# An expert stage on one core: in each slot the first-layer matmuls ahead of the second-layer matmuls of four slots back

## What is computed

```python
x = x + _L0_ffn_ref(_L0_cond_ref(x, cond, ...), ...)
# layer 1, the recurrence:
xw = einsum('ntd,dh->nth', x, Wx) + b
next_h = tanh(xw_t + prev_h @ Wh)               # 128 steps
# layer 1, the experts (E = 8, H = 128, F = 512):
router_logits = einsum('bth,eh->bte', x, router_w)
topk_values, topk_indices = top_k(router_logits, 2); topk_weights = softmax(topk_values)
h1 = gelu(einsum('bth,efh->btef', x, w1) + b1)
expert_outputs = einsum('btef,ehf->bteh', h1, w2) + b2
x = x + sum(topk_weights * take(expert_outputs, topk_indices))
```

## Time and profile before

| | us |
|---|---|
| median of 3 executions (305.28 to 305.82) | 305.47 |
| the profiled execution's own time | 305.9 |
| its span, first to last instruction | 304.1 |
| PE busy, 87% of the span | 265.9 |
| DVE busy, 85% | 259.6 |
| ACT busy, 71% | 216.3 |

### The profile page before, as it was taken

One profiled execution on the slowest core, in us unless ns is written; L12 is line 12 of the kernel. 1 busy time (PEld: TensorE's weight loads), 2 busy tenths in 40 slices (PEclk: granted clock), 3 DMA queues, 4 the chain that ended last, 5 costly groups with the idle time before them and its releaser, 6 DMA issues.

```text
span 304.1 us, 8645 instructions
## 1 busy us (share of the span) xinstructions
PE 265.9 (87%) x2716; PEld 205.2 (67%) x2716; DVE 259.6 (85%) x635; ACT 216.3 (71%) x455; POOL 74.6 (25%) x148
## 2 busy tenths in 40 slices
PE   4969950059989999999999999999999999999994
PEld 4724450026956877778888788888777877877873
DVE  4888999989898897879887789987789988899885
ACT  5368899997842667767777566667566766778882
POOL 3368996000025402010311122311110201101000
PEclk9979965558999999999999999999999999999999
DMA  6990544002500000000000001000001000001000
GB/s 178 325 300 4 98 95 77 8 0 52 88 0 2 1 2 1 0 2 9 11 0 0 2 2 29 0 0 0 1 2 28 8 0 0 2 1 38 0 2 26
DMA packets 24031, 10.62 MB, mean 35 GB/s; under 512 B 13356, under 2 KB 22983, under 8 KB 24007
## 3 DMA queue, kind: packets, MB, share of 16 engines
q1 hardware_dynamic: 23470, 10.05, 13.6%
q10 hardware_dynamic: 536, 0.26, 0.3%
HBM read 6.11 MB, written 1.05 MB: 24 GB/s over the span
## 4 chain that ended last, share of the span: by engine, by line
PE 74%; ACT 12%; DVE 8%; DMA 2%; issue 2%; ACTq 0%; DVEq 0%; SPq 0%
PE bank L891 73%; ACT big L518 2%; ACT big L516 2%; ACT big L525 2%; ACT big L521 2%; ACT big L532 2%; DMA wn<-in_w_gate 2%; DVE peak L631 1%; DVE big L742 1%; DVE wyT L825 1%; DMA y_sb<-in_cond 1%; ACT xT L466 1%; DVE big L870 0%; PE bank L1015 0%; DVE big L744 0%
## 5 line engine op out<-in xcount | busy, mean ns | idle before, releaser
L891 PE MATMUL bank<-big,wt 128*128 128x384 f16 (+2 forms) x480 | 124.7, 336 | 0.0
L891 PE MATMUL bank<-wt,big 128*128 (+1 forms) x1536 | 112.8, 219 | 1.4 <-DVE big L870 0.9
L870 DVE TENSOR_TENSOR big<-big 128x384 f16<-128x384 f32 (+2 forms) x160 | 93.3, 585 | 22.3 <-ACT big L592 18.2
L891 PEld LDWEIGHTS bank<-wt,big 128*128 128x128 f16 x1536 | 97.1, 97 | 19.8 <-issue 3.7
L590 ACT ACTIVATE big<-bank,miscT 128x384 f32<-128x384 f32 (+2 forms) x160 | 96.3, 603 | 11.2 <-PE bank L891 9.6
L891 PEld LDWEIGHTS bank<-q,wxh 128*128 128x128 f32 x254 | 44.8, 190 | 16.7 <-issue 2.8
L580 ACT ACTIVATE q<-bank (+1 forms) x112 | 20.6, 184 | 45.2 <-PE bank L891 44.4
L891 PEld LDWEIGHTS bank<-big,wt 128*128 (+1 forms) x480 | 49.6, 117 | 3.3
L404 POOL CAST big<-q 128x64 f16<-128x64 f32 x32 | 13.5, 423 | 133.3 <-ACT q L580 130.8
L866 DVE CAST big<-big 128x512 f16<-128x512 f32 (+2 forms) x104 | 38.8, 373 | 5.1 <-ACT big L590 4.6
L825 DVE SCALAR_TENSOR_TENSOR wyT<-bank,gates,wyT 128x128 f32<-128x128 f32 x128 | 39.8, 343 | 1.0 <-PE bank L891 0.4
(11 more groups left out here) (165 smaller groups left out, 312.4 us busy)
## 6 DMA issues: line engine op xcount, KB each, us to landing
wnat<-in_w SPq DMA_DIRECT2D x8, 512.0 KB, 7.7
x_sb<-in_x SPq DMA_DIRECT2D x4, 256.0 KB, 4.5
out_block<-wyT SPq DMA_DIRECT2D x15, 64.0 KB
wn<-in_w_gate ACTq DMA_DIRECT2D x1, 192.0 KB, 5.0
wn<-in_w_up SPq DMA_DIRECT2D x1, 192.0 KB, 5.9
wn<-in_w_down SPq DMA_DIRECT2D x1, 192.0 KB, 5.9
b_in<-in_b SPq DMA_DIRECT2D x12, 4.0 KB
wt<-wyT SPq DMA_TRANSPOSE x8, 3.0
```

What stands on the lines that cost most here:

```text
L870: V.tensor_tensor(g_lo[:, par, f, 0:w], g32[:, f, 0:w], g_hi[:, par, f, 0:w], ALU.subtract).then_inc(g_lo_done, 1)
L891: return nc.tensor.matmul(o, l, r, start=start, stop=stop, skip_group_check=True)
```

## The change

The down matmuls move, with their waits, into a function of their own, `earlier_slot`, which is called behind the slot's hidden matmuls; in a chunk's first slot (`first and s == 0`) it stays ahead of them. Since the hidden matmuls no longer stand behind the down wait, they get a wait of their own: that the gelu of four slots back has read the bank (`g32_done`), or, where ACT reads it twice, that `g_lo` is done. And the gelu gets a wait that `g_lo` of four slots back is done, so that `g32[f]` is free.

```diff
@@ ACT, pair @@
                     act.wait_ge(hid_mm, slot + 1)
                     bias = miscT[:, bass.ds(e2 * 2 * NF + s, 1)]
+                    if prev or s >= NF:
+                        act.wait_ge(g_lo_done, slot - NF + 1)
                     A(g32[:, f, 0:w], ps_h[f][:, 0:w], ACT.Gelu, bias=bias, scale=1 / WS).then_inc(g32_done, 1)
@@ PE @@
+            def earlier_slot(c, e2, prev, s):
+                first = is_first(e2)
+                f, par = s % NF, s // NF
+                slot = c * SLOTS + e2 * 2 * NF + s
+                if prev or s >= NF:
+                    e = e2 * 2 + par - 1 if not first else (E - 1 if par == 0 else 0)
+                    tiles = TILES[c - 1] if first and par == 0 else TILES[c]
+                    if f == 0 and prev:
+
+                        pe.wait_ge(added, added_before(c, e2, par))
+                    pe.wait_ge(g_lo_done, slot - NF + 1)
+                    down(e, 1 - par, f, tiles)
+
             def pair(c, e2, prev):
...
-                    if prev or s >= NF:
-                        e = e2 * 2 + par - 1 if not first else (E - 1 if par == 0 else 0)
-                        tiles = TILES[c - 1] if first and par == 0 else TILES[c]
-                        if f == 0 and prev:
-
-                            pe.wait_ge(added, added_before(c, e2, par))
-                        pe.wait_ge(g_lo_done, slot - NF + 1)
-                        down(e, 1 - par, f, tiles)
+                    if first and s == 0:
+                        earlier_slot(c, e2, prev, s)
                     step = rnn_step(c, e2, s)
...
+                    if prev or s >= NF:
+                        slot = c * SLOTS + e2 * 2 * NF + s
+                        two_reads = f in HI_SCALAR[c] or (first and f in HI_SCALAR[c - 1])
+                        pe.wait_ge(g_lo_done if two_reads else g32_done, slot - NF + 1)
                     t = slice(START[c], START[c + 1])
...
                     mm(o, w_hi, h_lo[:, t], False).then_inc(hid_mm, 1)
+                    if not (first and s == 0):
+                        earlier_slot(c, e2, prev, s)
```

More of the change, by code:

```diff
@@ L1086, in pair @@
                 for s in range(2 * NF):
-                    f, par = s % NF, s // NF
-                    slot = c * SLOTS + e2 * 2 * NF + s
+                    f = s % NF
                     if 0 < c < CH - 1 and first and s == 0:
```

## The result

| | before | after |
|---|---|---|
| median of 6 executions, us | 305.44 (304.90 to 305.92) | 302.15 (301.63 to 303.07) |
| ratio, 95% interval | | 0.9899 (0.9881 to 0.9918) |
| the profiled execution's own time, its span | 305.9, 304.1 | 303.04, 301.2 |

The change is 3.3 us faster by the medians, where 3.9 was forecast. By the two profiled executions it is 2.86. Such differences can lie ahead of the stage that was changed: in the fourteen profiled executions of this study `input_part` of chunk 0, the first row of the expert stage, starts at 99.1 to 99.7 us in four and at 100.3 to 100.8 in ten, whichever kernel it is. The executions without a profile have no rows, so where they differ isn't shown. The stage itself repeats closely: where a chunk's code was not touched, and neither was the chunk ahead of it, its length agrees to .02 us.

A forecast was written before the change was run, and what follows sets the result against it. PE was taken as the bound, with gains only at late starts: 1.15 + .66 + .86 + 1.0 + .43 - .2 = 3.9 us off 305.9 gives 302.0, and 301.6 for the median, .43 lower; range 300.4 to 303.8.

The forecast's parts named there:

- kind 4: Five places where PE's down matmuls wait for adds or `g_lo`, .14 to .28 each; all 1.0 us gained.
- chunk 0: Chunk 0 summed by its recurrence steps: gain 1.15 us, between .2 and 2.1.
- jumps: Chunk 1's two jumps back: the late sequencer mostly hidden behind queued matmuls, up to .1 staying; .66 gained, between .2 and .76.
- refill: Recurrence's bank at the ends of chunks 1 and 2: a down group fills the tanh wait, gaining .46 and .40.
- tail: The last 36 down matmuls, which lose .43 to the last two blocks' `g_lo`; all .43 gained.
- new waits: PE's and ACT's added waits ahead of hidden matmuls and gelu: a cost of .2 us in all.
- rival A: DVE holds chunk 0, jumps gain nothing, half of kind 4 comes back: 1.8 us gained, 303.7 us; chance .16.
- the first spacing: Chunk 0's step to step ahead of the first down matmuls: .80 instead of 1.34, without the wait for `g_lo`.
- the instructions in an expert's first slot: Chunk 0: one or two small instructions added between two steps, .1 for three slots a round, .3 in all.
- the loop's first round: Chunk 0's first loop round would take 6.17 like the others, where it took 6.48 while DVE is behind.
- the entry to the loop: Chunk 0, step to step where its loop begins: 1.10 instead of 1.30.
- Chunk 0 runs at the recurrence's pace: Chunk 0's loop: 1.05 us step to step, above PE's .81 of work, each step waiting for the previous tanh.

The follow-up runs named there:

- e4_chunk4: The kernel before, with the new order in chunk 4 alone (but for its first slot) and the new waits kept; 304.23 us, ratio to before .9957.
- e5_allglo: The changed kernel without ACT's new wait, and with PE's wait ahead of the hidden matmuls always for `g_lo`; 302.93 us, ratio to before .9919.
- e1_guard: The changed kernel, but chunk 0's choice of the new wait no longer looks at HI_SCALAR[-1], chunk 4's tuple; 302.42 us, ratio to before .9894.
- e2_drop: The changed kernel with one wait in place of two ahead of an expert's first down group; 301.84 us, ratio to before .9881.
- e6_waits: The changed kernel with three more wait instructions, long met, ahead of an expert's first down group; 306.34 us, ratio to before 1.0020.
- e11_before01: The kernel before, in its own order, with the loops of chunks 0 and 1 written out as straight code; 300.48 us, ratio to before .9842.
- e10_guard01: The changed kernel with chunks 0 and 1's loops written out and chunk 0's waits without HI_SCALAR[-1]; 298.04 us, ratio to before .9756.

## Why the prediction was right, and where it was not

The time, the range (300.4 to 303.8) and the sign held; the likeliest case was 301.6 and came out at 302.15. That is partly luck: the range is wide, and of the 2.54 forecast for chunks 0 and 1 only 1.27 came. In its own terms, by the lengths above, with kind 4's 1.0 split by chunks (.27, .14, .59):

| term | forecast | measured |
|---|---|---|
| chunk 0 | 1.15 | .35 |
| chunk 1: jumps .66, refill .46, wait for adds .27 | 1.39 | .92 |
| chunk 2: refill | .40 | .36 |
| chunk 3: wait for adds | .14 | .15 |
| chunk 4 and tail (.59 and .43) | 1.02 | 1.06 |
| new waits | -.2 | 0 (e4_chunk4, e5_allglo) |
| sum | 3.9 | 2.83 |

**Right: chunks 2 to 4 and the tail.** The reading of PE's starts, not of its busy share, gave these terms to within .04, and e4_chunk4 shows that chunk 4's is its own. DVE's share in chunk 4 didn't hold back half of it, as rival A had it. The busy time of the last 35 us of PE's matmuls (length, PE, PEld, DVE, ACT, POOL, clock), with the earlier trace rows:

```profile
262.25:297.25 35.00, 35.00 (x449) 28.60 (x446) 30.38 (x91) 29.59 (x61) 1.34 (x4) 1.00 0.04 9
```

PE issues 449 matmuls where it issued 434, and DVE is as busy as it was.

**Wrong: "the first spacing .80 instead of 1.34, since slot 4's hidden matmuls no longer wait for `g_lo`".** They do, by the index -1. It can be seen in the diff; the places of the program's order shown with it are in the loop. The term was .54; .25 came. e1_guard shows the cause, and that DVE takes back part of it later.

**Wrong in size: the instructions in an expert's first slot.** I counted .1 for three slots a round, .3 in all. Measured from step 0 to step 1 are .24, .21 and .18 more in the three rounds, and .19 together from step 4 to step 5: .82. The step that failed is the one on which instructions stand between which steps. I had priced the two waits as two small instructions; behind a jump they come in a stretch in which the sequencer is late already, and what the jump gained is partly spent there. In chunk 1, for which the forecast says that up to .1 stays, the same cost .14 and .18 behind the two jumps, so that these gained .32 and not .66. e2_drop and e6_waits, less and more of the same, move these spacings and nothing in chunks 2 to 4.

**Wrong: the loop's first round, "as 123.58 to 129.75, also for the first".** The first round takes 6.84, the others 6.48 and 6.36. About .36 of its .67 above the forecast's 6.17 are the instructions just named; the rest fits DVE, behind with the gates: in e1_guard a step that comes .37 earlier loses .27 in this round. That was part of rival A, which I had at .16.

**Better than forecast: the entry to the loop,** 1.29 to .80 where 1.10 stood in the sum. e5_allglo names the reason: the gelu is there earlier than `g_lo`. These .30 hide as much of the other misses in chunk 0: .29 at the first spacing, .52 of instructions and .31 in the first round.

**Right in place, too small a gain: the refill of chunk 1.** Row to row it lost .46 and loses .10. But e11_before01 shows that only .17 of chunk 1's gain needs the new order once the loop is gone; about .2 of the .46 was the way out of the loop (PE's timeline of that kernel, .43 from row to row where the earlier trace rows have .62):

```profile
163.03 0.32 PE L895 MATMUL bank<-big,wt 128*128 128x384 f16 x1
163.46 0.39 PE L895 MATMUL bank<-ones,bh_rows 33*128 33x512 f16 x1
```

**Right in place, cause misread: the waits for adds of kind 4.** Chunk 1's is this (the kernel before, DVE's and PE's timelines):

```profile
144.14 0.60 DVE L825 SCALAR_TENSOR_TENSOR wyT<-bank,gates,wyT 128x128 f32<-128x128 f32 x2
...
144.72 0.32 PE L891 MATMUL bank<-big,wt 128*128 128x384 f16 x1
145.00 0.82 PE L891 MATMUL bank<-wt,big 128*128 x9
```

The adds end at 144.75, and PE's turn for the down group is at 144.88, so the adds were not late; the group starts .25 behind their end. Likewise in the earlier trace rows: the adds end at 277.30, PE's turn is 277.34, the group starts at 277.55. The two others, at 235.12 and 272.87, have .25 and .27 from the adds' end to the group, and PE's turn lies between too. What stands in these .25 are two register instructions on PE's sequencer: the one with the wait starts at 277.340, 38 ns behind the adds' end, the next at 277.433, and the matmul at 277.554 (single records). In straight code (e11_before01) the adds of chunk 1 end .14 ahead of PE's turn as well, the group starts on time, and the spacing is 1.13 in both orders. So the new order covers the way from the wait to the matmul more than late adds.

**Half right: "Chunk 0 runs at the recurrence's pace".** In the loop it does; but of the 1.05 some .4 go with the loop's register instructions (last section), and that this could be had was not seen. In straight code step, tanh and the gaps between them add up to .29 + .04 + .18 + .05 = .56, and the .80 from step to step is PE's own work (.81 in the prediction). Step, tanh and step in the changed kernel's loop, then in straight code (e10_guard01), PE's and ACT's timelines:

```profile
119.01 0.37 PE L893 MATMUL bank<-q,wxh 128*128 x2
...
119.61 0.18 ACT L580 ACTIVATE q<-bank  x1
```

```profile
114.53 0.29 PE L897 MATMUL bank<-q,wxh 128*128 128x16 f32 x2
...
114.86 0.18 ACT L584 ACTIVATE q<-bank 128x16 f32<-128x16 f32 x1 [0.21 <-PE bank L897]
```

From the step to its tanh .60 in the loop, and .33 without it.

## What to carry to other kernels

Moving work behind work that doesn't depend on it pays only at the starts that are late, and these are read from the timeline's starts and not from busy shares; count for each place what stands between two steps after the move, on the sequencer too. In a loop whose body has short slots, waits and addresses that come from registers can be the bound: write it out and see, before the order inside it is tuned. An index that may become -1 in the first iteration is worth a look in every schedule that is written by chunk.

## What the runs showed of the hardware that I had not expected

**Register instructions behind a wait lie on the path of a chain, on both of its engines.** These are the instructions of line 580 (the recurrence's tanh) on ACT and its sequencer in the changed kernel's loop, from 119.3 to 119.9 us: count, ns, first and last start.

```profile
L580 ACTq FUSED_REGOPS  x1: 79/79/79, 119.4 to 119.4; - x1
L580 ACTq ALU_OP  x1: 35/35/35, 119.5 to 119.5; - x1
L580 ACT ACTIVATE q<-bank x1: 184/184/184, 119.6 to 119.6; - x1
```

The first one carries the wait for the step. In the single records of chunk 0's loop the tanh starts 228 ns after the step's end (median), in straight code 38; the next step starts 266 ns after the tanh's end at the least in the loop, and 52 in straight code. Together that is .4 of each 1.05 us. The Trainium skill, page "Perfetto Trace Analysis", section "Sequencer-only Instruction (DRAIN, etc)", has the sequencer hold at such an instruction's semaphore, execute, and only then fetch the next; the rows agree, since the second instruction starts behind the first.

**The same wait instructions cost .1 us each or nothing.** In chunks 0 and 1 three more cost .26 to .37 at nearly every place, in chunks 2 to 4 the lengths stayed the same to .01. What decides, as I read it, is whether matmuls are queued behind which the sequencer can be late (the earlier trace rows has it fourteen ahead in chunk 2); no run varies that alone. A wait that is met late takes this lead away, and then the instructions behind it show in chunks 3 and 4 too: the .25 behind adds above.

**Straight code was not slower.** Written out, chunks 0 and 1 save 4.65 us of the stage (196.80 to 192.15), and the first matmul of the stage comes no later (100.47 against 100.41, in the spread given above). That one chunk written out made the next one's loop .37 slower stays open.
